# Graph-attention kernel on one core: the last aggregation in groups of 16 slots, the small aggregation's store behind the next activations

## What is computed

```python
x = x + gnn0(layernorm(x), edges)        # 8 heads x 32 channels
x = x + ffn0(layernorm(x), edges2)       # an attention over a second edge list (4 heads x 4)
                                         # gates 4 experts, each gelu(x @ W1 + b1) @ W2 + b2
x = x + gnn1(layernorm(x), edges)        # 4 heads x 64 channels
x = x + ffn1(layernorm(x))               # 8 experts, top 2

# an attention layer, for each node i over its neighbours j (softmax over the neighbours of i):
score[i, j] = leaky_relu(mine[i] + neigh[j])          # one number a head
out[i]      = sum_j softmax_j(score[i, j]) * h[j]     # h[j]: H x C numbers
```

## Time and profile before

| what | us |
|---|---|
| median of 3 timed executions | 9118.57 (9118.34 to 9122.58) |
| the profiled execution: its own time, as its span from the first to the last instruction | 10110.4 |
| span minus median | 991.8 |
| first aggregation, first to last indirect transfer (in the profiled execution) | 1012.1 to 3648.0 |
| small aggregation, the same | 4255.4 to 5729.5 |
| last aggregation, the same | 6317.4 to 8733.1 |

### The profile page before, as it was taken

How to read it: one execution, slowest core, us unless ns; L and a number is a source line. 1 busy time by engine, 2 the same in 40 slices (tenths; PEclk the granted TensorE clock), 3 DMA queues, 4 the chain that set the end, 5 groups by cost and what they waited for, 6 DMA issues and landing times. The chain is left out here.

```text
span 10110.4 us, 54577 instructions
## 1 busy us (share of the span) xinstructions
PE 2288.8 (23%) x9111; PEld 1752.0 (17%) x9112; DVE 5594.3 (55%) x8828; ACT 1093.7 (11%) x2533; POOL 5337.1 (53%) x5411
## 2 busy tenths in 40 slices
PE   2112000000000002146555512000000000129995
PEld 1111000000000001135444411000000000116663
DVE  8764588788777677523333275455656556421111
ACT  1101000000000001112222201000000000002221
POOL 0025656666676654455555345776666777542221
PEclk7555555555555555578777755555555555559997
DMA  4051333433333353411111162433333333620004
GB/s 142 22 159 50 97 82 87 122 99 98 101 101 98 102 113 74 122 23 33 29 28 28 30 172 89 109 100 92 101 98 101 106 99 99 129 97 30 30 30 117
DMA packets 458121, 869.43 MB, mean 86 GB/s; under 512 B 175134, under 2 KB 294860, under 8 KB 448192
## 3 DMA queue, kind: packets, MB, share of 16 engines
q0 software_dynamic: 239536, 575.99, 23.0%
q1 hardware_dynamic: 167648, 182.04, 6.2%
q10 hardware_dynamic: 50788, 110.02, 3.3%
HBM read 693.35 MB, written 180.71 MB: 86 GB/s over the span
## 5 line engine op out<-in xcount | busy, mean ns | idle before, releaser
L914 POOL DMA_INDIRECT agg_ring<-table,agg_idx x4320 | 4275.8, 990 | 2329.8 <-issue 1323.4
L1042 DVE TENSOR_TENSOR agg_part<-agg_ring,agg_prob 128x2048 f32 x420 | 964.4, 2296 | 631.8 <-issue 556.2
L1080 DVE TENSOR_TENSOR agg_wide<-agg_wide,agg_part 128x2048 f32<-128x2048 f32 x420 | 960.4, 2287 | 14.4
L1786 PE MATMUL dense_tp<-all_ident,dense_xn 128*128 128x128 f32 x100 | 23.9, 425 | 2570.3 <-issue 2543.7
L1408 PE MATMUL agg_hp<-agg_xt,agg_w 128*128 128x256 f32 x1600 | 446.4, 439 | 579.4 <-ACT agg_ht L1378 340.3
L2208 DVE TENSOR_TENSOR experts_h<-experts_sg,experts_hp 128x682 f32<-128x682 f32 x106 | 91.8, 866 | 779.7 <-ACT experts_sg L2191 779.7
L2158 PE MATMUL experts_hp<-mixture_w,experts_xt 128*128 x1696 | 518.2, 458 | 0.6 <-ACT experts_xt L2187 0.6
L1408 PEld LDWEIGHTS agg_hp<-agg_xt,agg_w 128*128 128x128 f32 x1600 | 352.4, 224 | 663.8 <-ACT agg_ht L1378 360.4
L1786 PEld LDWEIGHTS dense_tp<-all_ident,dense_xn 128*128 128x128 f32 x100 | 20.3, 228 | 2571.9 <-issue 2544.5
L2129 POOL DMA_INDIRECT yc<-experts_ysb,experts_list x105 | 103.7, 987 | 685.2 <-DVE experts_ysb L2217 685.2
L1422 PE MATMUL agg_yp<-agg_w,agg_ht 128*128 128x256 f32 x1600 | 405.3, 411 | 231.0 <-remote 174.5
(11 more groups left out here) (421 smaller groups left out, 6520.8 us busy)
## 6 DMA issues: line engine op xcount, KB each, us to landing
agg_ring<-table,agg_idx POOLq DMA_INDIRECT x4320
y<-agg_ysb ACTq DMA_DIRECT2D x25, 1024.0 KB
rank_y<-y SPq DMA_DIRECT2D x10, 2560.0 KB
rank_x<-x SPq DMA_DIRECT2D x30, 640.0 KB
copies<-first_sort_words SPq DMA_DIRECT2D x16, 1024.0 KB
copies<-last_sort_words ACTq DMA_DIRECT2D x16, 1024.0 KB
x<-rank_x SPq DMA_DIRECT2D x20, 640.0 KB
agg<-agg_res ACTq DMA_DIRECT2D x98, 128.0 KB
```

Of the source, the lines that this page charges most:

```text
L914: pool.indirect_dma_start(out=self.ring[:, to:to + self.RW], out_offset=None, in_=self.table, in_offset=bass.IndirectOffsetOnAxis(ap=index ...
L1042: return dve.tensor_tensor(to[:, :].rearrange("p (j h c) -> p j h c", j=UNIT, h=H), ring[:, ds(st.at(at_u), UNIT * RW)].rearrange("p (j w) ...
L1080: dve.tensor_tensor(wide[:, :], wide[:, :], part[:, :], ALU.add).then_inc(widened, 1)
```

## The change

1. **The last aggregation** becomes a new function `aggregate`, the old one is renamed `aggregate_first` and is still used for list 0. The new one works in groups of `WIDE` = `SLOTS` = 16 slots: `wide` and `part` hold 16 x 256 = 4096 elements a partition, and `part` now lies in SBUF. The loop runs over whole groups and adds 2 to `taken` for each. The fold has one more step (`eighth`, 2048 elements). One-element memsets (`passed`) stand where the loop and its ends waited with a semaphore instruction, and more values are held in registers (`snap`). In ACT's part the loops count the same groups of 16.
2. The list of a tile's sizes holds 6 words of 16 bits in place of 5 of 32 (the first slot's number is split in two and put together again by register instructions). This holds for the first aggregation too.
3. `Cfg` has a smallest tile size, 16 slots for list 2 in place of 8.
4. In `SmallExperts.scalar` the store of the block before moves behind the Gelus of experts 0 and 1.

```diff
-        self.store(act, b - 1)                 # SmallExperts.scalar, half 0: from ahead of the Gelus
         for e in (0, 1) if half == 0 else (2, 3):
             ...
+        if half == 0 and not (isinstance(b, int) and b == 0):
+            self.store(act, b - 1)
...
+LOAD = 6
+WIDE = 16
+def aggregate(nc, cfg, H, C, table, info, ell, out, self_loop, S, beside):
+    UH, UC = SLOTS * H, SLOTS * CW
+        wide, part, folded_sum = s.sb("wide", [P, UC]), s.sb("part", [P, UC]), s.sb("folded_sum", [P, CW])
...
+                        dve.wait_ge(probs, kk)
+                        dve.memset(passed[:, 5:6], 0.0)
+                        weigh(g1, ending, wide).then_inc(tail, 1)
+                        dve.wait_ge(tail, kk)
+                        dve.memset(passed[:, 0:1], 0.0)
+                        with dve.Fori(g0, g1) as g:
+                            u = nc.s_assert_within(g - g0, 0, CH // SLOTS - 1, ...)
+                            so_far, weighed = dve.snap(g + 1), dve.snap(g * 2 + (cfg.RU + 1))
+                            dve.wait_ge(widened, so_far)
+                            dve.memset(passed[:, 6:7], 0.0)
+                            weigh(g, u, part).then_inc(taken, 2)
+                            dve.wait_ge(taken, weighed)
+                            dve.tensor_tensor(wide[:, :], wide[:, :], part[:, :], ALU.add).then_inc(widened, 1)
...
+                        dve.wait_ge(widened, g1 + 1)
+                        dve.tensor_tensor(wide[:, 0:8 * CW], wide[:, 0:8 * CW], wide[:, 8 * CW:16 * CW], ALU.add).then_inc(eighth, 1)
+                        dve.wait_ge(eighth, kk)
+                        dve.tensor_tensor(wide[:, 0:4 * CW], wide[:, 0:4 * CW], wide[:, 4 * CW:8 * CW], ALU.add).then_inc(quartered, 1)
...
-def aggregate(...)
+def aggregate_first(...)
-        sizes = s.sb("sizes", [1, 5 * (NT + 1)], I32)
+        sizes = s.sb("sizes", [1, LOAD * (NT + 1)], mybir.dt.uint16)
-            return nc.s_assert_within(ng, 1, CH, ...), nk, c0, k0, missing
+            return nc.s_assert_within(ng, 1, CH, ...), nk, c_high * SLOTS + c_low, k0, missing
...
-        (Cfg("2", 206250, 2048, 96), a["src"], a["dst"], None, 4, 64),
+        (Cfg("2", 206250, 2048, 96, SLOTS), a["src"], a["dst"], None, 4, 64),
```

More of the change, by code:

```diff
@@ L49, with __init__ @@
 class Cfg:
-    def __init__(self, name, E, F, RS):
+    def __init__(self, name, E, F, RS, least=UNIT):
         self.name, self.E, self.F, self.RS = name, E, F, RS
+        self.least = least
         self.RING, self.RU = RS // SLOTS, RS // UNIT
@@ L631, in _ @@
                 dve.wait_ge(md_made, 1)
-                ic.link(dve, dve.tensor_scalar(mdi[:, 0:NT], near[0:1, 256 + R0:256 + R0 + NT], 1.0, float(UNIT), ALU.add, ALU.max))
+                ic.link(dve, dve.tensor_scalar(mdi[:, 0:NT], near[0:1, 256 + R0:256 + R0 + NT], 1.0, float(cfg.least), ALU.add, ALU.max))
                 ic.link(dve, dve.tensor_scalar(ng, mdi[:, 0:NT], CH, None, ALU.min))
@@ L979, in aggregate, with aggregate_first @@
+def aggregate_first(nc, cfg, H, C, table, info, ell, out, self_loop, S, beside):
     CW = H * C
@@ L986, in aggregate @@
         ring, taken = st.ring, st.taken
-        sizes = s.sb("sizes", [1, 5 * (NT + 1)], I32)
+        sizes = s.sb("sizes", [1, LOAD * (NT + 1)], mybir.dt.uint16)
+        bits, split = s.sb("bits", [1, 2 * (NT + 1)], I32), s.sem("split")
         er, m, bm, mn = s.sb("er", [P, 2 * H]), s.sb("m", [P, H]), s.sb("bm", [P, H]), s.sb("mn", [P, H])
@@ L1005, in sizes_of @@
             why = "the ranking bounds every size of a tile"
-            ng, nk, c0, k0, missing = nc.values_load_multi_w_load_instructions(sizes[0:1, ds(t * 5, 5)], engines=[eng.engine], min_val=0, max_val=cfg.max_slots,
-                                                                      skip_runtime_bounds_check_because=why)[1]
-            return nc.s_assert_within(ng, 1, CH, skip_runtime_bounds_check_because=why), nk, c0, k0, missing
+            ng, nk, c_high, c_low, k0, missing = nc.values_load_multi_w_load_instructions(
+                sizes[0:1, ds(t * LOAD, LOAD)], engines=[eng.engine], min_val=0, max_val=cfg.max_slots, skip_runtime_bounds_check_because=why)[1]
+            return nc.s_assert_within(ng, 1, CH, skip_runtime_bounds_check_because=why), nk, c_high * SLOTS + c_low, k0, missing
         with nc.Block() as block:
@@ L1027, in _ @@
                 dve.wait_ge(st.info_in, 16)
-                of_tile = sizes[:, :].rearrange("p (t w) -> p t w", w=5)
+                of_tile = sizes[:, :].rearrange("p (t w) -> p t w", w=LOAD)
+                bits2 = bits[:, :].rearrange("p (t w) -> p t w", w=2)
+                dve.tensor_scalar(bits2[:, :, 0], st.inf[:, I_C0:I_C0 + NT + 1], 4, None, ALU.logical_shift_right).then_inc(split, 1)
+                dve.tensor_scalar(bits2[:, :, 1], st.inf[:, I_C0:I_C0 + NT + 1], SLOTS - 1, None, ALU.bitwise_and).then_inc(split, 1)
                 dve.tensor_scalar(of_tile[:, :, 0], st.inf[:, I_NG:I_NG + NT + 1], 1.0, None, ALU.max).then_inc(sized, 1)
-                dve.tensor_scalar(of_tile[:, :, 4], st.inf[:, I_NK:I_NK + NT + 1], -1.0, 4096.0, ALU.mult, ALU.add).then_inc(sized, 1)
-                for w, first in ((1, I_NK), (2, I_C0), (3, I_K0)):
-                    dve.tensor_copy(of_tile[:, :, w], st.inf[:, first:first + NT + 1]).then_inc(sized, 1)
+                dve.tensor_copy(of_tile[:, :, 1], st.inf[:, I_NK:I_NK + NT + 1]).then_inc(sized, 1)
+                dve.tensor_copy(of_tile[:, :, 4], st.inf[:, I_K0:I_K0 + NT + 1]).then_inc(sized, 1)
+                dve.tensor_scalar(of_tile[:, :, 5], st.inf[:, I_NK:I_NK + NT + 1], -1.0, 4096.0, ALU.mult, ALU.add).then_inc(sized, 1)
+                dve.wait_ge(split, 2)
+                dve.tensor_copy(of_tile[:, :, 2:4], bits2[:, :, :]).then_inc(sized, 1)
                 dve.wait_ge(const, 5)
@@ L1369, in scalar @@
     def scalar(self, act, b, half):
-        if half == 0 and not (isinstance(b, int) and b == 0):
-            self.store(act, b - 1)
         for e in (0, 1) if half == 0 else (2, 3):
@@ L2325, in build @@
                 share = Beside([(sorts[1], 0, len(sorts[1].so.steps), 0, 17), (sorts[2], 0, EARLY, 17, NT)])
-                aggregate(nc, lists[0][0], 8, 32, tabs[0], infos[0], ells[0], outs[0], True, S, share)
+                aggregate_first(nc, lists[0][0], 8, 32, tabs[0], infos[0], ells[0], outs[0], True, S, share)
             rank(1, after=sorts[2], done=EARLY, beside=dense[1])
```

179 lines of the change are left out of this document (added).

## The result

| | median us | lowest to highest | runs |
|---|---|---|---|
| before, beside it | 9119.65 | 9118.34 to 9122.58 | 4 |
| after | 9564.58 | 9559.99 to 9570.25 | 4 |

The ratio is 1.0489, with a 95% interval of 1.0476 to 1.0502: the change costs 445 us. The forecast was 9586, +467 us.

What follows compares the result with a forecast made beforehand. POOL's queue of indirect transfers, one every 1.25 us, was taken to set the timed stages' pace. 9118.6 + 459 (holding) + 5 (sizes) + 4 (tail) = 9586 us, +5.1%; range 9400 to 9690. Profiled span forecast: about 10,428 us.

Steps and rivals of the forecast that it cites:

- The reading of the gap: Profile span 991.8 us above timed median: taken as POOL's 929 us of waits for DVE, absent when timed.
- Part 1, the holding: Last aggregation: DVE additions and folds with two SBUF inputs hold POOL's transfers; 384 + 75 = 459 us.
- The formula: Delay of a held transfer: DVE instruction's duration minus 0.14 us minus how far in it was issued, on average 0.62.
- Rival D: Each addition catches its transfer early, as one hold sets the next's phase; up to 9710 us; chance 0.08.
- The test of the formula on the kernel before: Formula gives 40 us for existing short instructions in 48 tiles; rows have about 100, so it does not overstate.
- What part 1 saves: Loop in groups of 16, last aggregation: taken as nothing, bound -146 us, POOL's waits for DVE.
- part 2's bounds of 0 and 36: Six-word sizes load and slot-number register instructions in the first aggregation: 5 us taken, bounds 0 and 36.
- Part 4: Store behind two experts' Gelus, small aggregation: 0 at POOL's pace; bound -133 us, half of ACT's 266 us wait.
- The tail: The last tile's longer tail after POOL is done: +4 us.
- A: POOL is held, but timed executions also have the DVE waits, which go: 9440 us, with part 4's bound 9307; chance 0.12.
- B: No holding for such additions: the index read slips in, POOL keeps its pace, 9119 to 9124 us; chance 0.05.
- C: DVE paces the last aggregation and the loop's saving comes out: -146 us, 8973 us; chance 0.05.

Runs made afterwards that it cites:

- the old loop: The changed kernel with its last aggregation calling `aggregate_first` (units of 8, `part` in PSUM), parts 2 to 4 kept; 9146.47 us, 1.0014 of before.
- the first experiment: Part 1 taken back in the changed kernel: last aggregation calls `aggregate_first` (units of 8, `part` in PSUM), parts 2 to 4 kept; 9146.47 us, 1.0014 of before.
- the third experiment: As the first experiment, but `part` lies in SBUF in the last aggregation; 9458.57 us, 1.036 of before, +312 us over the first experiment.
- the sixth experiment: As the first experiment, but the first slot's number is kept in a register once a tile instead of worked out at each use; 9134.01 us, 1.0018 of before.
- the ninth: As the first experiment, but sizes are five 16-bit words with the slot's number whole, and DVE loads only four; 10054.73 us, 0.9946 of before.
- the eleventh: The ninth plus, in the last aggregation, a one-reduction fold and `er`, `mn`, folded sum in PSUM, with the store ahead of the Gelus again; 10111.82 us, 1.0003 of before.

## Why the prediction came out right

**The reading of the gap.** "In the timed executions register instructions are short" held for the chips on which before takes 9120 us; POOL's waits for DVE in the last aggregation are 9 us in the old loop there. But that 929 us of waits lay near 992 was partly luck. Between the profile of before and the first experiment's, the stages shrink by 190, 388 and 227 us, and 172 us more go outside them, which the sum had not counted; in exchange some 200 us of waits stay in the first aggregation. That "all three stages go at POOL's pace" was true of two of them.

**Part 1, the holding.** Right in mechanism, in place and nearly in size. Here is each transfer's lengthening over 0.946 us, put down to the DVE instruction whose end lies 0.81 us ahead of its own, and summed over the last stage from the traces:

| | additions | us, each | folds of 2048 | us, each | stage us |
|---|---|---|---|---|---|
| forecast | 105 | 384, 3.66 | 49 | 75, 1.53 | |
| after | 105 | 358, 3.41 | 48 | 96, 2.00 | 2624.6 |
| addition reads PSUM | | 0 | 48 | 70, 1.47 | 2245.1 |
| groups in two halves, PSUM | | 0 | 48 | 76, 1.58 | 2257.5 |
| old loop, `part` in SBUF | 209 of 2048 | 288, 1.38 | | | 2506.9 |

After has 459 us of lengthening in all, the old loop 23; the difference is the 436 us by which the stage grew. The forecast's 459 was the gross figure, and that the gross sum came out to the microsecond is luck: additions and folds make 454 of it, one term 26 us too high and the other 21 too low, and short instructions the rest. It also missed that the 23 us of holds of the old loop (13 of them by its folds of 1024 elements, in 42 tiles) would go. The two terms are off in opposite ways, both by the phase. The formula took a transfer 0.62 us into the addition on average. In fact the hold of one addition sets the phase of the next. The held transfer ends 0.82 us after the addition, the next ones start 1.13, 2.38, 3.63 and 4.88 us after it, and the next addition of the same loop starts 4.88 us after it too (7022.41 to 7027.29 in the timeline above). So in 56 of the 105 a transfer starts within 0.02 us of the addition and slips through, and the one held is the next, 1.25 us in; in the other 49 the held one starts 0.34 us in or later. The mean is 0.91. And the fold begins at a set distance, 0.97 us, behind the last addition's end. The held transfer ends at a set distance behind it too, and the next one is issued 1.13 us behind it, so 0.16 us into the fold, not 0.62. With the addition freed the phase is loose again and the fold costs 1.47 and 1.58, as forecast. Rival D had this thought, but the phase that the holds set is early for the folds and late for most additions. In the third experiment the 209 additions held 288 us where 321 were expected; the folds of 1024 elements made up for it, with 45 us in place of 13, again 0.16 us in.

The test of the formula on the kernel before was no test. The "some 100 us" of lengthening are there (100.5 us), but only some 26 of them end 0.81 us after a DVE instruction; the other 74 are spread over some 400 transfers, most of them longer by 0.15 us, and in the first experiment, with short register instructions, they are gone (0.04 us). So the formula's 40 us for the short instructions stood against 26 and 23 us: it overstated them. What made those 74 stays open.

That what is held is the transfer's read of its indices is not shown either. No run moved the indices; the runs show the place of the DVE inputs and the 0.81 us.

**What part 1 saves** was rightly taken as nothing. DVE's busy time of 1626 us ("about 1600") lies under POOL's pace, and 858 us of DVE's idle time in the stage bought nothing.

**Parts 2 to 4** together cost 13 us (1.0014 [1.0004, 1.0023]) in the first experiment, within part 2's bounds of 0 and 36 and above the 5 taken. The load of six words takes DVE 1.49 us in after:

```profile
L1231 DVEq TENSOR_LOAD <-agg_sizes x49: 1383/1486/4405, 983.4 to 3366.7; - x49
```

Against the 1.19 of the earlier trace rows that is 0.30 x 49 = 15 us, in the one stage where POOL waits for DVE; it fits, and the sixth experiment leaves little else. Shown alone it is not: the ninth shortened the load with part 4 in place, and on a chip where the eleventh, with short loads too, is no faster than before. That the 1.19 were taken in the other condition is a further caution. Part 3 changed no count: the last aggregation has 1728 transfers before and after.

**Part 4**: 0 within the interval, as forecast at POOL's pace. On a chip where register instructions are long the waits are on the path and it gives 67 us, half of the bound of 133.

**The tail** was forecast as +4 us. From the last transfer to the end of the aggregation DVE takes 10.5 us after and 18.3 in the first experiment, so it gives 8 us back. With 436, 13 and -8 the sum is 441, against 445 measured.

**The rivals.** A falls: after was timed and profiled with short register instructions, and there were no waits in the last stage to be replaced. B falls with the 4.88 us transfer, and the statement of the Trainium skill behind it ("SBUF — State Buffer", section "Who interferes with whom", that `tensor_tensor` did not stall software-issued DMA) does not hold for these indirect transfers: 0.94 us beside the addition with one input in PSUM, 4.88 beside the same one with both in SBUF. Its other statement, on two SBUF inputs against a GpSimd read, is what the experiments show, though for the whole length in one direction only: a transfer that came first cost the addition 0.03 to 0.05 us, not its own 0.94. C falls: the old loop waits for DVE 9 us in the stage, so there was no 146 us to save, and two forms of the groups of 16 in which the additions hold nothing are still slower than the old loop (1.0078 and 1.0085 against 1.0014), by about what their longer fold holds (70 and 76 us, less the 13 of the old one). D's 555 us were not reached.

**What the signs said.** Transfers up to 5.2 us: 4.90. Mean about 1.27: 1.214. Additions 4.42, ends 0.8 us later, waits near zero, DVE idle ahead of the scores: all seen. The stage of 2650 to 2750 us was 2624.6; that sign had been worked out from the profile of before with its waits, the condition after's profile was not in. For the same reason the span of 10,428 us was not seen.

## What to carry to other kernels

When one engine's queue of short instructions sets a stage's end, ask of every long instruction on the other engines not only how busy it makes them but which memory its inputs lie in: moving one scratch buffer from PSUM to SBUF cost 312 us here with no instruction added. An instruction longer than the queue's interval catches one of the queue's instructions nearly every time, for more than half of its own length: 209 additions of 2.29 us cost 288 us of holds, 105 of 4.42 us cost 358, so merging them did not help. And before a profile's waits are priced, its execution's time is held against the timed ones: where they differ by a tenth, a wait in it may not exist in the time that is asked for, and an edit can be worth 67 us in one condition and nothing in the other.

## What the runs showed of the hardware that was not expected

The register instructions and branches of DVE's sequencer take about 50 ns on some chips; on others they take as little from 1000 to 2000 us, and mostly 700 ns and up to 1400 in the last aggregation. The kernel before has a median of 9118 to 9133 us in three of the comparisons here and of 10,095 and 10,103 in the two others. What decides it stays open. A transfer that is issued within 0.02 us of the start of an addition with two SBUF inputs gets through, and the addition then takes 4.45 to 4.47 us in place of 4.42: there the delay goes the other way, by some 0.03 to 0.05 us.
